# Target rows of the message stage kept as three bf16 terms instead of one fp32 row

## The reference

```
src_feats, dst_feats = x[src], x[dst]
h1 = relu(concat([src_feats, dst_feats, edge_attr]) @ W1.T + b1)
messages = h1 @ W2.T + b2
aggregated = segment_sum(messages, dst)
r, z = sigmoid(i_r + h_r), sigmoid(i_z + h_z)      # gi from aggregated, gh from x
n = tanh(i_n + r * h_n)
x = layernorm(x + (1 - z) * n + z * x)
```

## Time and profile before

| | us |
|---|---|
| median of 3 runs | 6299.3 (6287.5 to 6302.6) |
| profiled execution | 6231.5 |
| its span on the core | 6229.8 |
| PE / DVE / ACT / POOL busy in it | 4549.0 / 2780.5 / 1293.4 / 3203.0 |
| granted clock of TensorE, mean | 0.833 |

### The profile page before, as it was taken

The page is one execution under the profiler, slowest core; times in us unless marked ns, Lnnn a source line. Parts: engine busy times, 40 slices in busy tenths (PEclk is TensorE's granted clock), DMA queues, the critical chain, the costliest instruction groups (busy, mean ns, idle before and its releaser), DMA issues. The chain is left out here.

```text
span 6229.8 us, 76164 instructions
## 1 busy us (share of the span) xinstructions
PE 4549.0 (73%) x26200; PEld 3101.7 (50%) x26200; DVE 2780.5 (45%) x7313; ACT 1293.4 (21%) x2474; POOL 3203.0 (51%) x3381
## 2 busy tenths in 40 slices
PE   4551374886876777678879988998787466777776
PEld 3330232443543555554446655666554366666665
DVE  6770385673435676545551215123323233343435
ACT  1130362000016655211120002001100111122222
POOL 4557303656746566155516643663564456565552
PEclk7665686997987899889989999999898677787788
DMA  5252278886871334275578869787864444444442
GB/s 149 34 49 20 38 125 142 169 173 135 171 141 49 101 89 114 69 227 158 164 238 245 250 209 287 235 243 239 246 201 154 110 112 115 113 122 112 120 119 73
DMA packets 1272757, 913.03 MB, mean 147 GB/s; under 512 B 453955, under 2 KB 1193582, under 8 KB 1272286
## 3 DMA queue, kind: packets, MB, share of 16 engines
q1 hardware_dynamic: 914474, 523.11, 34.0%
q0 software_dynamic: 109744, 232.50, 13.9%
q10 hardware_dynamic: 248132, 152.25, 8.5%
HBM read 698.11 MB, written 121.01 MB: 131 GB/s over the span
## 5 line engine op out<-in xcount | busy, mean ns | idle before, releaser
L1640 PE MATMUL ps<-adj_d,xs_d 128*128 128x464 bf16 (+1 forms) x4704 | 1045.6, 378 | 101.7 <-DVE xs_d L1601 72.7
L3119 POOL DMA_INDIRECT rows_mg<-p_tab,src_idx x784 | 755.7, 964 | 526.4 <-DVE pre_mg L3168 259.8
L1554 POOL DMA_INDIRECT rows_d<-xh_tab,src_idx x632 | 614.0, 971 | 566.3 <-POOLq L188 205.0
L1261 POOL DMA_INDIRECT rows_d<-h_tab,slot_idx x490 | 492.8, 1006 | 611.8 <-POOLq L188 382.4
L1554 POOL DMA_INDIRECT rows_d<-x_tab,src_idx x512 | 503.3, 983 | 543.5 <-POOLq L188 255.5
L1640 PEld LDWEIGHTS ps<-adj_d,xs_d 128*128 128x128 bf16 x4704 | 476.4, 104 | 595.7 <-issue 123.5
L1048 PE MATMUL ps<-hot,lo 128*128 128x459 bf16 (+5 forms) x1250 | 349.5, 403 | 439.5 <-DVE hot L921 189.1
L2169 POOL DMA_INDIRECT rows_g<-x_tab,src_idx x444 | 432.3, 974 | 266.8 <-issue 113.6
L1397 PE MATMUL ps<-adj_d,xs_d 128*128 128x512 bf16 (+1 forms) x2028 | 477.2, 388 | 117.3 <-issue 67.2
L1626 PEld LDWEIGHTS ps<-onehot_d,rows_d 128*128 128x128 f32 x3552 | 442.0, 196 | 97.5 <-issue 76.9
L1626 PE MATMUL ps<-onehot_d,rows_d 128*128 128x72 f32 (+1 forms) x3552 | 438.2, 278 | 60.6 <-issue 54.3
(11 more groups left out here) (440 smaller groups left out, 7587.6 us busy)
## 6 DMA issues: line engine op xcount, KB each, us to landing
adj_d<-adjacency SPq DMA_DIRECT2D x140, 812.0 KB
adj_d<-adjacency SPq DMA_DIRECT2D x84, 857.5 KB
attr_mg<-in_edge_attr SPq DMA_DIRECT2D x195, 256.0 KB
xp_g<-x_tab SPq DMA_DIRECT2D x70, 448.0 KB
k_rows_d<-k_tab ACTq DMA_DIRECT2D x56, 448.0 KB
loc_mg<-loc_rows SPq DMA_DIRECT2D x196, 128.0 KB
q_s<-q_tab SPq DMA_DIRECT2D x42, 448.0 KB
rden_s<-rden_tab SPq DMA_DIRECT2D x42, 448.0 KB
```

Source lines behind the costliest of these rows:

```text
L1261: nc.gpsimd.indirect_dma_start(rows[:, v % RW, k, :], None, table, bass.IndirectOffsetOnAxis(ap=slot_idx[:, j:j + 1], axis=0)).then_inc(ro ...
L1554: nc.gpsimd.indirect_dma_start(rows[:, q % GR * K + k, :], None, table, bass.IndirectOffsetOnAxis(ap=src_idx[:, j:j + 1], axis=0)).then_in ...
L1640: last = nc.tensor.matmul(ps[:, m % 2, 0:w], xs[:, g * GW + k, e, :], adj[:, slot, k, 0:w], start=(g == 0 and k == 0 and e == 0), stop=(g ...
L3119: nc.gpsimd.indirect_dma_start(rows[:, q % RR, k, :], None, p_tab, bass.IndirectOffsetOnAxis(ap=src_idx[:, j:j + 1], axis=0)).then_inc(row ...
```

## The change

A new table q3_terms holds each target row as three bf16 rows (TERMS = 3): the row rounded to bf16, the rest rounded, and the rest of that. layer2_last makes them: ACT copies q_rows to bf16 (high_term), POOL subtracts that from q_rows (first_rest), ACT rounds the rest (middle_term), POOL subtracts again, into bf16 (second_rest), and SP writes all three (put_terms, three parts behind). The lags are 6 and 7. POOL's loads of share become work at lag 0 of the same list. A blank block fills the rows from NP to AW. In the message stage `win` holds three terms (96 KB a group in place of 64), the one-hot is bf16, and the single fp32 product with `win` becomes three bf16 products into the same bank. q3_tab is still written.

```diff
--- before.py
+++ after.py
@@ -242,7 +242,7 @@
         q_tab = dram("q_tab", [HEADS * P, NP])
         rden_tab = dram("rden_tab", [HEADS * P, NP])
         p_tab = dram("p_tab", [NP, P])
-        q3_tab = dram("q3_tab", [AW, P])
+        q3_tab, q3_terms = dram("q3_tab", [AW, P]), dram("q3_terms", [AW, TERMS, P], BF16)
 
 
         W0 = [0, 1, 2]
@@ -2832,13 +2832,17 @@
                     return st.enter_context(nc.sbuf_tensor(f"{name}_t", shape, dt))
                 share = tmp("share", [P, 3, BLOCK])
                 rows, p_rows, q_rows = [tmp(k, [P, 2, BW, P]) for k in ("rows", "p_rows", "q_rows")]
+                rest, terms = tmp("rest", [P, 2, 1, BW, P]), tmp("terms", [P, 2, BW, TERMS, P], BF16)
+                blank = tmp("blank", [P, TERMS, P], BF16)
                 stats, mean_var = tmp("stats", [P, 2, BW, 6]), tmp("mean_var", [P, 2, BW, 2])
                 sd, rstd, shift = [tmp(k, [P, 2, BW]) for k in ("sd", "rstd", "shift")]
                 names = ["halved", "final", "turned", "taken", "measured", "rooted", "inverse", "shifted", "normed", "back", "in_place",
-                         "product", "p_copied", "q_made", "p_out0", "p_out1", "q_out0", "q_out1", "share_in0", "share_in1", "share_in2"]
+                         "product", "p_copied", "q_made", "high", "left", "middle", "low", "p_out0", "p_out1", "q_out0", "q_out1", "terms_out0",
+                         "terms_out1", "blank_made", "blank_out", "share_in0", "share_in1", "share_in2"]
                 with stage(*names) as (block, halved, final, turned, taken, measured, rooted, inverse, shifted, normed, back, in_place,
-                                       product, p_copied, q_made, p_out0, p_out1, q_out0, q_out1, *share_in):
-                    p_out, q_out = (p_out0, p_out1), (q_out0, q_out1)
+                                       product, p_copied, q_made, high, left, middle, low, p_out0, p_out1, q_out0, q_out1, terms_out0,
+                                       terms_out1, blank_made, blank_out, *share_in):
+                    p_out, q_out, terms_out = (p_out0, p_out1), (q_out0, q_out1), (terms_out0, terms_out1)
 
                     def steps(*works):
 
@@ -2890,6 +2894,7 @@
                             dve.wait_ge(p_copied, j + 1)
                             if j >= 2:
                                 dve.wait_ge(q_out[j % 2], 16 * (j // 2))
+                                dve.wait_ge(left, j - 1)
                             nc.vector.tensor_tensor(q_rows[:, j % 2, 0:nw, :], pair(j, nw, 1), bias_rows[:, 2:3, :].to_broadcast([P, nw, P]),
                                                     ALU.add).then_inc(q_made, 1)
 
@@ -2952,23 +2957,61 @@
                                 act.wait_ge(p_out[j % 2], 16 * (j // 2))
                             nc.scalar.copy(p_rows[:, j % 2, 0:nw, :], pair(j, nw, 0)).then_inc(p_copied, 1)
 
-                        steps((3, put), (2, scale), (1, root), (4, source_rows))
+                        def high_term(j, c, nw):
+                            act.wait_ge(q_made, j + 1)
+                            if j >= 2:
+                                act.wait_ge(terms_out[j % 2], 16 * (j // 2))
+                            nc.scalar.copy(terms[:, j % 2, 0:nw, 0, :], q_rows[:, j % 2, 0:nw, :]).then_inc(high, 1)
+
+                        def middle_term(j, c, nw):
+                            act.wait_ge(left, j + 1)
+                            nc.scalar.copy(terms[:, j % 2, 0:nw, 1, :], rest[:, j % 2, 0, 0:nw, :]).then_inc(middle, 1)
+
+                        steps((3, put), (2, scale), (1, root), (4, source_rows), (6, high_term), (7, middle_term))
 
                     @block.gpsimd
                     def _(pool):
-                        for j, (c, nw) in enumerate(parts):
+                        nc.gpsimd.memset(blank[:, :, :], 0.0).then_inc(blank_made, 1)
+
+                        def share_row(j, c, nw):
                             if j >= 3:
                                 pool.wait_ge(halved, j - 2)
                             pool.dma_start(share[:, j % 3, 0:nw * P], dinv_row[c:c + nw * P].partition_broadcast(P)).then_inc(share_in[j % 3], 16)
 
+                        def first_rest(j, c, nw):
+                            pool.wait_ge(high, j + 1)
+                            if j >= 2:
+                                pool.wait_ge(low, j - 1)
+                            nc.gpsimd.tensor_tensor(rest[:, j % 2, 0, 0:nw, :], q_rows[:, j % 2, 0:nw, :], terms[:, j % 2, 0:nw, 0, :],
+                                                    ALU.subtract).then_inc(left, 1)
+
+                        def second_rest(j, c, nw):
+                            pool.wait_ge(middle, j + 1)
+                            nc.gpsimd.tensor_tensor(terms[:, j % 2, 0:nw, 2, :], rest[:, j % 2, 0, 0:nw, :], terms[:, j % 2, 0:nw, 1, :],
+                                                    ALU.subtract).then_inc(low, 1)
+
+                        steps((0, share_row), (6, first_rest), (7, second_rest))
+
                     @block.sync
                     def _(sp):
+                        def put_terms(j, c, nw):
+                            sp.wait_ge(low, j + 1)
+                            sp.dma_start(q3_terms[c:c + nw * P, :, :].rearrange("(k p) e f -> p k e f", p=P), terms[:, j % 2, 0:nw, :, :]
+                                         ).then_inc(terms_out[j % 2], 16)
+
+                        sp.wait_ge(blank_made, 1)
+                        sp.dma_start(q3_terms[NP:AW, :, :], blank[:, :, :]).then_inc(blank_out, 16)
                         for j, (c, nw) in enumerate(parts):
                             sp.wait_ge(p_copied, j + 1)
                             sp.dma_start(p_tab[c:c + nw * P, :].rearrange("(k p) f -> p k f", p=P), p_rows[:, j % 2, 0:nw, :]).then_inc(p_out[j % 2], 16)
                             sp.wait_ge(q_made, j + 1)
                             sp.dma_start(q3_tab[c:c + nw * P, :].rearrange("(k p) f -> p k f", p=P), q_rows[:, j % 2, 0:nw, :]).then_inc(q_out[j % 2], 16)
-                        for sem in (*p_out, *q_out):
+                            if j >= 3:
+                                put_terms(j - 3, *parts[j - 3])
+                        for j in range(len(parts) - 3, len(parts)):
+                            put_terms(j, *parts[j])
+                        sp.wait_ge(blank_out, 16)
+                        for sem in (*p_out, *q_out, *terms_out):
                             sp.wait_ge(sem, 16 * G)
 
         class Finish:
@@ -3093,8 +3136,9 @@
                 def tmp(name, shape, dt=F32):
                     return st.enter_context(nc.sbuf_tensor(f"{name}_mg", shape, dt))
                 rows, attr, onehot = tmp("rows", [P, RR, K, P]), tmp("attr", [P, RA, K, P]), tmp("onehot", [P, OH, K, P])
-                win, loc = tmp("win", [P, RA, P]), tmp("loc", [P, RA, K * P], I16)
-                turned_hot, attr_T, pre, hid = [tmp(k, [P, 2, K * P]) for k in ("turned_hot", "attr_T", "pre", "hid")]
+                win, loc = tmp("win", [P, RA, TERMS, P], BF16), tmp("loc", [P, RA, K * P], I16)
+                turned_hot = tmp("turned_hot", [P, 2, K * P], BF16)
+                attr_T, pre, hid = [tmp(k, [P, 2, K * P]) for k in ("attr_T", "pre", "hid")]
                 finish = Finish(tmp)
                 names = [f"rows_in{k}" for k in range(RR)] + [f"group_in{k}" for k in range(RA)]
                 names += ["cleared", "matched", "located", "turned", "copied", "mixed", "met", "rectified", "summed", "added", "rest_in"]
@@ -3135,7 +3179,7 @@
                                          ).then_inc(group_in[b], 16)
                             if whole < K:
                                 sp.dma_start(attr[0:REST, b, whole, :], edge_attr_128[FULL * P:E, :]).then_inc(rest_in, 16)
-                            sp.dma_start(win[:, b, :], q3_tab[bass.ds(base[q % GU], P), :]).then_inc(group_in[b], 16)
+                            sp.dma_start(win[:, b, :, :], q3_terms[bass.ds(base[q % GU], P), :, :]).then_inc(group_in[b], 16)
                             sp.dma_start(loc[:, b, :], loc_rows[q * K:(q + 1) * K, :].rearrange("t p -> (t p)").partition_broadcast(P)
                                          ).then_inc(group_in[b], 16)
 
@@ -3213,7 +3257,8 @@
                                 pe.wait_ge(met, q - 1)
                             for k in range(K):
                                 c = slice(k * P, (k + 1) * P)
-                                nc.tensor.matmul(ps[:, 2 + q % 2, c], turned_hot[:, q % 2, c], win[:, q % RA, :], start=True, stop=False)
+                                for e in range(TERMS):
+                                    nc.tensor.matmul(ps[:, 2 + q % 2, c], turned_hot[:, q % 2, c], win[:, q % RA, e, :], start=(e == 0), stop=False)
                                 end = nc.tensor.matmul(ps[:, 2 + q % 2, c], attr_T[:, q % 2, c], wt(W3[2]), start=False, stop=True)
                             end.then_inc(mixed, 1)
```

## The result

The changed kernel takes 6392.9 us (median of 4 runs, 6374.8 to 6393.9), the kernel before in the same set of runs 6296.3 (6287.5 to 6302.6): ratio 1.0155, 95% interval 1.0138 to 1.0172, **slower by 97 us**. The forecast was 6412 us in a range of 6340 to 6465.

What follows compares the result with a forecast made beforehand. No engine was full: a count of PE instructions per POOL stretch bounded the message stage, a chain through in-order engines layer2_last. 92 + 21 = +113 us on 6299.3 gave 6412 us, own range 6358 to 6466, widened down to 6340.

Steps and rivals of the forecast that it cites:

- layer2_last, +92 forecast: Stage making the terms: added copies, subtractions and held share loads lengthen it, 53 + 11 + 28 = +92 us, bounds +72 to +130.
- +53 and +11: In layer2_last: share rows 8 to 13 at 14.0 us instead of 5.2, +53; row 7, first behind a subtraction, +11.
- The tail: End of layer2_last, last share addition to next stage's first gather: 51 us instead of 23.5, +28.
- PE's part: In a layer2_last step: PE turns, then multiplies, until ACT's copy can begin, 3.4 and 1.9 us, mean 2.65.
- the ring's terms: In layer2_last: share load, additions, statistics, scaling, PE, copies, subtractions and handovers close a circle of 14.0 us a step.
- The rival in which the share loads aren't held: layer2_last: POOL's queue issues share loads while subtractions wait; stage +41 us, kernel 6361; chance 0.12.
- The message stage, +21 forecast: Message stage: 74 POOL waits of 3.8 us, 281 against 260, +21 us; bounds -13 to +37.
- the rival in which the count doesn't matter: Message stage: slack phases come from something PE's instructions don't feed; 92 - 13, kernel 6378; chance 0.15.
- count of PE instructions per stretch of POOL work: Message stage: PE gets 65 to 84 products before it slackens; 32 for 28 a group makes 65 stretches 74.
- The win product: Message stage: three bf16 products take 0.20 us for one fp32 product's 0.22; 1 us on the path, dropped.
- The one-hot in bf16: Message stage, on a pause's path: from 495 ns to about 0.37 us.
- The faster rival: Message stage: PE's work in fp32 passes runs out and bf16 relieves it; up to 260 us off, 6131; chance 0.10.

Runs made afterwards that it cites:

- e1_share_ahead: The changed kernel with a buffer and semaphore for each of the 14 share rows, all loaded at the head of POOL's program: 6358.2 us, 1.0098.
- e7_one_term: The changed kernel with only the first of three bf16 terms multiplied in the message stage, 24 records a group: 6392.8 us, 1.0115.
- e4_pool_pause: The kernel before with a 1000-column memset (0.95 us) on POOL, waited for, after each group's four gathers: 6166.5 us, 0.9793.
- e2_terms_unused: The changed layer2_last with the message stage of the kernel before; terms are written and not read: 6386.1 us, 1.0135.
- e8_six_tiny: The kernel before with six 8-column fp32 products more per group of the message stage, 40 records for 28: 6388.8 us, 1.0124.

## Why the prediction was right

**layer2_last, +92 forecast, +91.8 measured.** Its parts, too. Share rows 8 to 13 were to come 14.0 us apart: load 7 starts at 4860.75, the last at 4947.95, so 87.2/6 = 14.5. Between the first and the last share addition it was +53 and +11; the rows give 121.7 us for 57.2, +64.5. The tail was to be 51 us; it is 50.1 (4951.2 to 5001.3), +26.6 for +28. The missing 0.7 us lies before the first share addition, which starts 4.1 us after its load for 3.4. The terms of one turn:

```profile
L2990 POOL TENSOR_TENSOR terms_t<-rest_t,terms_t 128x512 bf16<-128x512 f32 x7 | 8.1, 1153 | 0.0
...
L2985 POOL TENSOR_TENSOR rest_t<-q_rows_t,terms_t 128x384 f32<-128x384 f32 x7 | 6.4, 912 | 56.3 <-ACT terms_t L2964 56.3
...
L2964 ACT CAST terms_t<-q_rows_t 128x512 bf16<-128x512 f32 x7 | 4.3, 620 | 10.5 <-DMA q_terms<-terms_t 10.5
```

A subtraction is 1.03 us in the mean, not 1.25; GPSIMD Engine Reference in the Trainium skill, Elementwise, with 0.97 by its 2.6 cycles, was nearer than my row. Two of them give 0.4 us a turn back. PE's part took more in its place: ACT waited for it before the p copy ten times, 34.7 us, so 3.5 each for the 2.65 that I took; the granted clock was 0.63 for 0.76, and a product of 256 columns took 540 ns for 454. So the two errors in the ring's terms offset each other, which is luck. The rival in which the share loads aren't held is out: the loads stand behind the subtractions. Its number, +41 for the stage, is what e1_share_ahead shows when they are really not held (+40.4), and by its own parts: +9 between the additions, +31 behind the last.

**The message stage, +21 forecast.** The number of waits came out (75 for 74), and the two profiles differ by 22 us. That the two agree is partly luck: a wait didn't get shorter (3.98 us for 3.8 forecast), so the waits grew by 38.6 us and not by 21, and POOL's own gathers and gaps took 16 us less (749.8 and 219.5 for 755.7 and 229.9). And the medians don't settle the term: they leave 96.6 - 91.8 = 5 us in the changed kernel and 22 in e1_share_ahead, with the same message stage. If the 5 us are right, the term was too large by some 16, which is the distance of the forecast's 113 from the measured 97; the runs can't tell that from noise. Nor can the total tell the forecast from the rival in which the count doesn't matter: 6393 lies 19 us under the one and 15 above the other (6378). And the step under it, "a **count of PE instructions per stretch of POOL work**", failed as a law: e7_one_term took a quarter of the records out and kept 70 waits, ACT stood for 11 us before a copy that had all it needed, and on the third chip PE doesn't slacken. e4_pool_pause, which broke POOL's stretches and emptied the list of waits, bears out only its second half, the stretch of POOL work. What holds in its place is narrower: on two of three chips PE's pace, and at times ACT's, falls while POOL issues indirect transfers without a break, more work on PE makes more pauses, less work doesn't clearly make fewer. Which property of the chip, or of its state at that time, it hangs on, stays open, for each chip ran one group; no row shows what "issue" is waiting for. Runtime: NRT & Kernel Launch in the Trainium skill, Instruction fetch mechanics, has fetching hidden by the issue floor. The third chip would agree, the first two would not if fetching is what PE waits for; no run here shows that it is.

**The win product**, 0.20 us for 0.22, was right in that it didn't matter, and off in size: a tile's five products take 0.44 us as before. TensorE: Matmul & The Clock Gate in the Trainium skill, Back-to-back issue gap, gave 0.24 for the three, 0.46 with the attr pair, and the trace's 0.44 lies between that and my 0.42. The one-hot in bf16 is 370 ns in the mean (72.5 us over 196), as forecast, for 495 before. No wait of PE for windows appears. DVE's waits in front of the one-hot (578 us) are put down to a long-finished load of share rows, but each of the 129 waits between 5050 and 6150 us ends within 0.3 us of one of SP's attribute loads, which the same `mixed` of PE releases. So they are waits for PE, and the wider transfer was rightly costed at nothing.

**The faster rival** falls: PE's work in fp32 passes isn't what runs out. In e2_terms_unused the fp32 products stand behind the same new layer2_last, and the pauses are no more than with the terms (68 for 75).

## What to carry to other kernels

A transfer issued from a computing engine waits in that engine's program behind all compute put in front of it, though it needs nothing from it. When work is added to such an engine, walk once around the ring of buffers; here the walk gave 92 us and the profile 91.8, and giving the loads buffers of their own took 51 of them back. And before a remedy for a stall that the profile only calls "issue" is kept, time it on a second chip: a pause was worth 2.1% on one chip, and on another even a smaller one cost 2.4%.

## What was not expected of the hardware

- The same program took 6296, 6306 and 5327 us on three chips. The difference is spread over the run and shows as PE's "issue" time, which all but vanishes on the third. From 500 to 700 us PE has 72 records on the first two and 1105 on the third.
- Where PE slackens, a 0.95 us fill on GpSimd behind every four indirect gathers (1.25 us each) takes the long slack phases away and gains 129 us; 0.45 us every four, or 0.95 us every eight, gains 14 and 28.
- An fp32 product of 8 columns isn't nearly free: in e8_six_tiny 12 records (six products) a group added 217 us of PE's modelled busy time over 196 groups, 0.18 us a product.
